# The router's steps in another order in a fused decoder layer: statistics ahead of token residuals, the logit product behind the combiner product, the routing in two parts

## What is computed

```
x = x + attn(layernorm(x))          # linear: Q = x.qw, pre = Q.x, attn = pre.x, out = attn.combiners, 4 heads of 128
x = x + xattn(layernorm(x), ctx)    # q, k, v products, softmax(q k / sqrt(512)) v
x = x + ffn(layernorm(x))
ffn(t) = t-shared-mlp + sum of 2 experts:
  logits = t @ router_w + router_b; probs = softmax(logits); vals, idx = top_k(probs, 2); vals /= sum
  pos = running count of the expert over all tokens - 1; within = pos < 640; scatter, 16 expert mlps (704 wide), gather
```

## Time and profile before

| | |
|---|---|
| median of 3 runs | 1967.63 us |
| profiled execution | 1968.63 us, span 1966.9 us |
| phase 1 | to about 610 us, a round takes 71.5 us |
| TensorE busy | 97% |
| DVE, ACT, POOL busy | 42%, 34%, 41% |

### The profile page before, as it was taken

How to read it: one execution, slowest core, us unless ns; L and a number is a source line. 1 busy time by engine, 2 the same in 40 slices (tenths; PEclk the granted TensorE clock), 3 DMA queues, 4 the chain that set the end, 5 groups by cost and what they waited for, 6 DMA issues and landing times.

```text
span 1966.9 us, 27705 instructions
## 1 busy us (share of the span) xinstructions
PE 1909.5 (97%) x10672; PEld 1686.7 (86%) x10672; DVE 822.1 (42%) x1896; ACT 666.9 (34%) x1366; POOL 807.6 (41%) x662
## 2 busy tenths in 40 slices
PE   8999999999999999999999999999999999999997
PEld 5788788788777778888899999999999999999996
DVE  2566576576674322222223333333333333333332
ACT  3344444444443211111243333333333333334321
POOL 2133143143164220000455655656546566556531
PEclk9999999999999999999999999999999999999999
DMA  7020330330335432233445544555444455445522
GB/s 273 3 103 27 129 109 21 129 129 7 132 132 171 107 66 65 66 94 72 112 114 123 125 99 120 129 118 123 109 106 129 117 129 116 96 128 124 122 33 27
DMA packets 106738, 203.40 MB, mean 103 GB/s; under 512 B 14800, under 2 KB 14800, under 8 KB 106352
## 3 DMA queue, kind: packets, MB, share of 16 engines
q1 hardware_dynamic: 81312, 148.52, 24.1%
q0 software_dynamic: 25296, 53.11, 15.4%
HBM read 135.92 MB, written 65.68 MB: 102 GB/s over the span
## 4 chain that ended last, share of the span: by engine, by line
PE 67%; DVE 1%; ACT 1%; issue 0%; POOL 0%; ACTq 0%; DVEq 0%; POOLq 0%
PE ps L70 43%; PE ps L1250 22%; PE ps L1192 2%; ACT buffer L1068 0%; DVE buffer L1141 0%; DVE buffer L1156 0%; DVE stats L483 0%; ACT buffer L349 0%; PE ps L662 0%; ACT buffer L1106 0%; PE ps L668 0%; POOL out_tokens L1057 0%; ACT L1106 0%; ACT lg L409 0%; DVE buffer L1181 0%
## 5 line engine op out<-in xcount | busy, mean ns | idle before, releaser
L70 PE MATMUL ps<-buffer,buffer 128*128 128x320 f32 (+1 forms) x6816 | 1223.2, 340 | 6.6 <-DVE buffer L564 2.1
L70 PEld LDWEIGHTS ps<-buffer,buffer 128*128 128x128 f32 x6816 | 1105.1, 188 | 111.6 <-issue 3.3
L1012 POOL TENSOR_TENSOR buffer<-buffer,buffer 128x512 fp32r<-128x512 f32 x289 | 387.4, 1503 | 229.1 <-ACT buffer L1068 228.7
L1250 PE MATMUL ps<-buffer,buffer 128*128 128x512 f32 x1904 | 458.7, 396 | 4.9 <-DVE buffer L1141 4.9
L1250 PEld LDWEIGHTS ps<-buffer,buffer 128*128 128x128 f32 x1904 | 352.2, 189 | 78.3 <-issue 3.9
L1156 DVE TENSOR_TENSOR buffer<-ps,buffer 128x320 f32<-128x320 f32 (+1 forms) x240 | 127.5, 532 | 602.5 <-ACT buffer L1106 600.8
L1106 ACT ACTIVATE buffer<-ps 128x320 f32<-128x320 f32 (+1 forms) x240 | 112.3, 468 | 655.1 <-PE ps L70 655.1
L1068 ACT ACTIVATE buffer<-buffer 128x512 fp32r<-128x512 f32 (+3 forms) x529 | 269.6, 563 | 56.7 <-PE ps L1250 50.5
L1057 POOL DMA_INDIRECT out_tokens<-buffer,slot_index x80 | 125.5, 1569 | 220.0 <-DVE buffer L1181 207.3
L1141 DVE TENSOR_TENSOR buffer<-buffer,buffer 128x320 fp32r<-128x320 f32 (+1 forms) x240 | 186.0, 775 | 12.0 <-ACT buffer L1068 10.8
L316 POOL TENSOR_TENSOR buffer<-buffer,buffer 128x512 fp32r<-128x512 f32 x32 | 41.1, 1316 | 316.5 <-ACT buffer L344 316.5
(11 more groups left out here) (109 smaller groups left out, 958.3 us busy)
## 6 DMA issues: line engine op xcount, KB each, us to landing
buffer<-in_wts SPq DMA_DIRECT2D x289, 256.0 KB, 2.8
tokens_normed_T<-buffer SPq DMA_DIRECT2D x16, 1024.0 KB, 8.7
buffer<-tokens_normed_T SPq DMA_DIRECT2D x16, 1024.0 KB, 6.5
buffer<-in_x SPq DMA_DIRECT2D x8, 1024.0 KB, 6.6
buffer<-in_ctxT SPq DMA_DIRECT2D x8, 1024.0 KB, 12.7
tokens_normed<-buffer SPq DMA_DIRECT2D x8, 1024.0 KB, 4.5
out_tokens<-buffer SPq DMA_DIRECT2D x8, 1024.0 KB, 4.3
out_tokens<-buffer POOLq DMA_DIRECT2D x32, 256.0 KB, 3.9
```

What stands on the lines that cost most here:

```text
L70: last = pe.matmul(out, left, right, start=(i == 0), stop=(i == len(todo) - 1))
L1012: pool.tensor_tensor(wl[n % RING][:], wraw[n % RAW][:], wh[n % RING][:].bitcast(F32), ALU.subtract).then_inc(s_wl, 1)
L1250: ins = pe.matmul(down_bank[n % 2][:], left, right, start=(c == 0 and i == 0), stop=(c == FC - 1 and i == len(passes) - 1))
```

## The change

The list of a round gets another order, on all engines at once: LN0(i+1) ahead of Y2T(i-1); LP(i-1) behind T(i+1); LX(i-1) behind SC(i); L(i-1) in two steps, L1 behind LX (bias, row maximum, exponentials) and L2 behind LN1(i+1) (everything else); X(i-1) behind PV(i). y2l gets rows of its own, so that the ring of weights and a few waits change with it. In phase 2 the parts of the last batch's router move by a unit.

```
-    y2l_rows = [at(8, [NC, S], F32R)] * (B - 2) + [at(38, [NC, S], F32R), at(52, [NC, S], F32R)]
+    y2l_rows = [at(42, [NC, S], F32R)] * (B - 1) + [at(52, [NC, S], F32R)]
...  ACT, step G
-                if b >= 2:
-                    act.wait_ge(s_ytout, 32 * (b - 1))
...  DVE, step Y2T
+                if b >= 1:
+                    dve.wait_ge(s_ytout, 32 * b)
...  DVE: L becomes L1, and behind the row maximum
+            if name == "L2":
                 dve.wait_ge(s_le, NT * (b + 1))
...  PE, V
+                drained(pe, "X", b - 2)
...  PE, LP
+                drained(pe, "T", b + 2, 2)
...  PE, T
-                drained(pe, "LX", b - 2)
...  PE, X
-                drained(pe, "T", b + 2, 0)
+                drained(pe, "A", b + 2, 1)
...  PE, PT
+                drained(pe, "LX", b - 1)
...  PE, A
-                drained(pe, "X", b - 2)
...
-        steps = [("Y1T", i), ("V", i), ("KROW", i), ("Y2T", i - 1), ("LN0", i + 1), ("INIT", i + 1), ("Q", i),
-                 ("LP", i - 1), ("G", i + 1), ("LX", i - 1), ("T", i + 1), ("L", i - 1), ("WV", i + 1), ("QB", i + 1),
-                 ("SC", i), ("X", i - 1), ("M", i + 1), ("PT", i),
-                 ("C", i + 1), ("A", i + 1), ("LN1", i + 1), ("SCATTER", i - 1), ("PV", i), ("LN2", i)]
+        steps = [("Y1T", i), ("V", i), ("KROW", i), ("LN0", i + 1), ("Y2T", i - 1), ("INIT", i + 1), ("Q", i),
+                 ("G", i + 1), ("T", i + 1), ("LP", i - 1), ("WV", i + 1), ("QB", i + 1),
+                 ("SC", i), ("LX", i - 1), ("L1", i - 1), ("M", i + 1), ("PT", i),
+                 ("C", i + 1), ("A", i + 1), ("LN1", i + 1), ("L2", i - 1), ("SCATTER", i - 1), ("PV", i),
+                 ("X", i - 1), ("LN2", i)]
...
-    router = {(0, 2): [("Y2T", B - 1)], (0, 3): [("LP", B - 1)], (0, 4): [("LX", B - 1), ("L", B - 1)],
-              (1, 0): [("X", B - 1)]}
+    router = {(0, 2): [("Y2T", B - 1)], (0, 3): [("LP", B - 1)], (0, 4): [("LX", B - 1), ("L1", B - 1)],
+              (0, 5): [("L2", B - 1)], (1, 1): [("X", B - 1)]}
```

More of the change, by code:

```diff
@@ L404, in step @@
                 copy(logits_T[:], bank[:]).then_inc(s_ev["LP"], 1)
-            if name == "L":
+            if name == "L1":
                 act.wait_ge(s_lg, b + 1)
@@ L916, in ring_slot_free @@
         elif n < 18:
+            filled(eng, "Y1T", B - 1, NC - 1)
+            eng.wait_ge(attn["s_krow"], B)
+        elif n < 20:
             filled(eng, "LP", B - 2)
@@ L1042, in gpsimd @@
                     split(n)
-                if (g, c) == (1, 1):
+                if (g, c) == (1, 2):
                     step("SCATTER", B - 1)
@@ L1223, in tensor @@
                     ins.then_inc(s_gu, 1)
-                    if (g, c) == (1, 0):
+                    if (g, c) == (1, 1):
                         pe.wait_ge(s_ost, NT)
```

## The result

The changed kernel takes 2023.93 us, the median of 4 runs (2022.07 to 2024.32); the kernel before took 1967.2 us beside it (1965.84 to 1968.98). The ratio is 1.0286 [1.0268, 1.0304]: slower by 57 us. The forecast was 2028 (1997 to 2044). The profiled execution has a span of 2020.4 us.

The account below looks back on a forecast made before the run. TensorE, busy 1909.5 of 1966.9 us, was taken as the bound, so only its waits count. Terms 22.1 (G and order), 23.4 (L2), 9 (clock) and 4.9 (round 7) sum to 59.4 on 1968.6: 2028 us, range 1997 to 2044.

Parts of the forecast that it names:

- G's new time: Gram product G starts 2.1 us later, at v + 30.6 (v: V's start), after waiting 7 us for y2l.
- From G to the next round: From G's start to the next V: net +1.3 us up to SC, +0.06 for LX, +0.47 for X, each round.
- L2: Second routing part on DVE, held by POOL's bias adds: V 3.9 us later in 6 rounds, 23.4 us.
- The clock: TensorE's clock falls behind G's 7 us wait each round: 13.8 us lost, less 4.7 already lost before, +9.
- Case (c): Rival: the clock falls before V as well, X and Y1T running in pieces: 6 x 2.5 more, 2044 us; chance 0.07.
- Round 7 and the join: Last round and shared expert: LX's wait -2.0, PT's copies +0.6, third unit net +3.2, last unit +1.65; together +4.9 us.
- (a): Rival: L2's small operations pass beside POOL without being held, 2002 us; chance 0.25.
- (b): Rival: POOL's y2 adds come behind krow's start, G 3.9 us earlier in rounds 2 to 6, 2003 us; chance 0.06.
- (d): Rival: G doesn't wait at all, about 26 us go, 1943 us; chance 0.06.
- the 22.1: Rounds 1 to 6, G's later start and the way to the next V: 3.9 us a round, 2.6 in round 1.

Follow-up runs that it names:

- the kernel made for it: The changed kernel with POOL's SCATTER behind its y2 adds instead of ahead of them: 2001.6 us, ratio 1.0177.
- the last kernel: Kernel before with SCATTER late, y2l's own rows, T's wait, round 7's weight copies and last routing moved, LN0 ahead of Y2T except on ACT: 1939.33 us.

## Why the prediction was right, point by point

- **G's new time.** Said: v + 30.6, 7 us behind Q, for y2l. Found: v + 31.1, 7.30 us, L523, by the chain named (krow held, statistics, y, y2h, y2l). The size of krow's hold was said to be about 4 us and was 4.95. G's late start has two causes, and each is shown by undoing it alone: ACT's order 3.1 us of G's start and 18 us of the kernel, SCATTER's place 3.4 us and 22 us.
- **From G to the next round.** Said: +1.3. Found: 1.06 (3.79 less G's own 2.73). For the new places of LX and X I had 0.53 more. It doesn't show: from SC's start to the next V it takes 3.5 us more, and 3.5 is what L2's hold alone is worth.
- **L2.** Said: held by POOL's run, V 3.9 us later. Found: 3.5. I had the one-hots wait for the end of the run and the rest follow it; but one operation is let in at each end of a POOL instruction, and picked is through together with the run. X waits 1.42 us, not 2. The term was 23.4, and 3.5 x 6 is 21, the same in the kernel with L2 early and in the one without POOL's adds.
- **The clock.** Said: 13.8 us lost behind G's waits, +9. Found: 12.7. Before, by the same records of G (6.78 and 5.31 us in rounds 2 and 3), it was 4.4, so +8.3. Of the 12.7, 2.8 are round 1's, and four other kernels with the same order up to there didn't lose them: this part can be chance of the profiled execution. Case (c) happens in two of six rounds and has no price, since V's 0.8 us there only shorten G's wait.
- **Round 7 and the join.** Said +4.9, found 5.8, and here the nearness is partly luck. LX's 2.54 went, LP's and SC's 1.17 came (said: net -2.0, found: -1.4). Up to the third unit it comes to +1.8 (said: +3.2). Behind it, two last down projections wait 1.58 and 2.91 where one waited 2.86 (said +1.65, found +1.6), and the lower clock takes 1.6 us in the third unit and 0.8 in the down projections, for which the prediction had no term.
- **The rivals.** (a) is refuted by the kernel without bias adds. (b) did not occur, and the kernel made for it shows its price nearly right: 2003 said, 2001.6 measured, with G 3.4 us earlier instead of 3.9. (d), no wait of G, needs the other order on ACT and POOL: it is what the last kernel has.

The Trainium skill (SBUF — State Buffer, Who interferes with whom) has a DVE instruction with two SBUF inputs and a GpSimd one that reads SBUF exclude each other for a whole instruction. The trace agrees: 2.52 against 0.36 us for the one-hots, at the boundaries of POOL's 1.25 us. That the krow product is held over four such instructions (4.95 us) goes beyond this sentence.

The sum, by the starts of V in the two profiled executions: V of round 1 stands at 118.65 (before: 120.90, 2.2 later, which the change doesn't explain). From there to V of round 7 the six rounds take 48.9 us more (8.0, 5.6, 7.6, 9.9, 8.5, 9.4), where the terms of these rounds had 54.5. In parts, over the six rounds:

| | said | found |
|---|---|---|
| G's start behind V | 11.3 | 13.4 |
| G's own records, by the clock | 9 | 8.3 |
| from G to SC, without G's records | 7.8 | 6.4 |
| from SC to the next V (L2, and X and LX) | 26.6 | 20.8 |
| sum | 54.7 | 48.9 |

The said values are those of the prediction, the 22.1 split up (with its rounding 54.5). So the largest miss is L2's term, 2.4 too large, with the 3.2 for the places of X and LX; G's start was put too early. Rounds 2 and 3 show less than the others because before, too, the clock fell in them. Round 7 and the join add 5.8 (said: 4.9), up to the end of the down projection, at 717.41 where it was 664.98. With 1.1 behind it that is the span's 53.5. Between the medians lie 56.7 us: the profiled execution of the changed kernel (2022.07) is the shortest of its four, 1.9 below their median, and that of before (1968.63) 1.4 above its own.

Two expectations failed, for one kind of reason. L2 behind L1 (2000 said, 2008.9 found) meets POOL's weight splits in round 7; SCATTER late alone (1950 said, 1960 found) meets ACT's wait for the transfers. In the one I had read the order for rounds 2 to 6 only, in the other for the compute engines only. Not settled: why the transfers hold ACT in three rounds and not in the others.

## What to carry to other kernels

In a list that all engines walk through, a step moved for one engine's sake is moved on all: read, for each engine, which copy or eviction now stands behind a late one, and give that engine its own order (the swap of two steps costs 22 us by itself; with a loop on ACT that keeps its old order, and SCATTER late, it gains 5). Before short DVE work with two SBUF inputs is put anywhere, look at what POOL does at that time; a run of POOL instructions can also be moved, and moving eight SCATTERs behind four adds was worth 22 us in one kernel and 7 in another. A wait of TensorE costs more than its length when the clock falls behind it.

## What was not expected of the hardware

- Not every operation gets in between POOL's instructions. POOL's four adds behind one another take 5.01 us, whether DVE waits or not. Of DVE's small operations (128x64 and 128x8) one gets in at each end of a POOL instruction: 0.77, two in 2.52 and 1.18 us. A 128x512 krow product, in the same kernel beside an equal run, waits for all of what is left of the run: 4.95 us, with 4.4 of POOL's run ahead of it; the longest of the 32 took 7.46 us. It is not the kind of operation, for a 128x512 subtraction (L1147) at 670.56 took 4.97 us. Nor is it the size alone, for the same subtraction at 750.25, amid five POOL instructions behind one another, got in at the next end: it took 1.28 us, and POOL's instruction behind it 1.72. What decides it is open.
- One wait, two clocks. In round 1 G waits 2.98 us in the changed kernel and in four made from it (L2 early, SCATTER late, Q repeated, no bias adds). G's records take 6.65 us in the first and 3.81 in the four. SCATTER, L2 and the repeated matmuls come only behind this place, so three of the four have run the same instructions up to there. The length of the wait alone does not decide whether the clock falls.
- Small operations with one tensor input are held too. The cast of 128x8 took 0.77 us beside POOL and 0.17 without; in the kernel with L2 early the 128x4 TENSOR_SCALAR took 1.23 us, where it takes 0.17 in round 4.
- More matmuls made the kernel faster. With 27 us of repeated products ahead of G's waits it took 13.6 us less. 10 us of it are shown to be theirs: G then ran in 3.81 us at a granted clock of 1.00 instead of 5.14 to 6.57.
